# Row maxima of an attention kernel made 80 units ahead instead of 104, and some of their row transfers moved to ScalarE's queue

## The reference, cut to what matters

```python
xn = layernorm(x)                        # x: (2, 2048, 512)
q, k, v = split(xn @ W_qkv)              # 16 heads of 32
a = q @ k.T / sqrt(32) + alibi + causal  # per batch and head: 2048 x 2048
y = softmax(a) @ v
attn = y @ W_o
ffn = top-1 of 8 experts on xn           # gate * (xn @ W[e].T + b[e])
out = x + attn + ffn
```

## Time and profile before

| | us, or as said |
|---|---|
| median of 3 runs | 1774.7 (1774.01 to 1775.14) |
| the profiled execution | 1770.8 |
| its span | 1769.0 |
| PE busy | 1666.7 (94%) |
| DVE busy | 1045.4 (59%) |
| ACT busy | 761.1 (43%) |
| POOL busy | 675.0 (38%) |
| packets on ScalarE's queue q10 | 4608, for 32 y stores |
| idle of PEld until an exp of ACT | 86.4 in 365 waits, 0.8 the longest |

### The profile page before, as it was taken

The page is one execution under the profiler, slowest core; times in us unless marked ns, Lnnn a source line. Parts: engine busy times, 40 slices in busy tenths (PEclk is TensorE's granted clock), DMA queues, the critical chain, the costliest instruction groups (busy, mean ns, idle before and its releaser), DMA issues. The chain is left out here.

```text
span 1769.0 us, 27986 instructions
## 1 busy us (share of the span) xinstructions
PE 1666.7 (94%) x9970; PEld 1011.5 (57%) x9971; DVE 1045.4 (59%) x2452; ACT 761.1 (43%) x1575; POOL 675.0 (38%) x643
## 2 busy tenths in 40 slices
PE   5999999679999999999999999999999998799898
PEld 4777777444545545554555554554554533688686
DVE  5433332467777766776766776776776700634366
ACT  2222222114554654655655555555555564411110
POOL 4500000004862553553554454454355365223350
PEclk9999999859999999999999999999999999899999
DMA  6655564571803703702801801900900500545596
GB/s 228 215 180 184 178 205 147 161 127 39 157 8 71 124 8 65 137 8 53 148 8 41 160 8 30 171 8 20 182 8 8 202 7 13 173 143 164 189 395 229
DMA packets 96927, 203.59 MB, mean 115 GB/s; under 512 B 10908, under 2 KB 28348, under 8 KB 91164
## 3 DMA queue, kind: packets, MB, share of 16 engines
q1 hardware_dynamic: 82984, 170.17, 36.9%
q0 software_dynamic: 9216, 23.47, 4.2%
q10 hardware_dynamic: 4608, 8.39, 1.6%
HBM read 122.46 MB, written 79.01 MB: 114 GB/s over the span
## 5 line engine op out<-in xcount | busy, mean ns | idle before, releaser
L1037 ACT ACTIVATE probs_sb<-score_ps 128x512 f32<-128x512 f32 (+3 forms) x1280 | 595.1, 546 | 486.5 <-PE score_ps L1106 223.7
L916 POOL TENSOR_TENSOR pair_sum<-probs_sb 128x512 f32<-128x512 f32 x384 | 480.7, 1284 | 422.0 <-ACT probs_sb L1037 333.4
L939 DVE TENSOR_REDUCE part_max<-max_ps 128x1 f32<-128x512 f32 x768 | 476.0, 679 | 248.3 <-PE max_ps L1071 248.0
L1071 PE MATMUL max_ps<-k_aug,q_aug 104*128 104x512 f32 (+3 forms) x1280 | 531.4, 427 | 27.2 <-DMA q_aug<-q_rows_d 19.8
L1103 PE MATMUL score_ps<-q_aug,k_aug 106*128 106x512 f32 (+3 forms) x1280 | 475.2, 392 | 13.0 <-DMA q_aug<-max_lo 8.9
L1071 PEld LDWEIGHTS max_ps<-k_aug,q_aug 104*128 104x128 f32 x1280 | 250.7, 197 | 183.7 <-issue 80.4
L1103 PEld LDWEIGHTS score_ps<-q_aug,k_aug 106*128 106x128 f32 x1280 | 243.7, 191 | 114.4 <-ACT probs_sb L1037 86.4
L1148 PE MATMUL acc_ps<-probs_sb,v_sb 128*32 128x512 f32 (+3 forms) x2560 | 291.1, 534 | 0.0
L935 DVE CUSTOM_DVE_ANT_0 max_ps<-max_ps,mask_row 128x384 f32<-128x384 f32 (+3 forms) x512 | 238.8, 514 | 48.7 <-PE max_ps L1071 45.5
L1148 PEld LDWEIGHTS acc_ps<-probs_sb,v_sb 128*32 128x32 f32 x2560 | 73.0, 110 | 118.1 <-issue 91.3
L623 DVE SCALAR_TENSOR_TENSOR st_lo<-group_ps,st_hi 128x512 fp32r<-128x512 f32 x64 | 44.3, 692 | 139.9 <-ACT st_hi L670 139.9
(11 more groups left out here) (175 smaller groups left out, 1737.9 us busy)
## 6 DMA issues: line engine op xcount, KB each, us to landing
k_aug<-k_hi_d SPq DMA_DIRECT2D x14, 1024.0 KB
q_aug<-q_hi_d SPq DMA_DIRECT2D x14, 1024.0 KB
slot_y_d<-y_rows SPq DMA_DIRECT2D x39, 256.0 KB, 2.0
xn_d<-xn SPq DMA_DIRECT2D x8, 1024.0 KB, 5.4
q_hi_d<-st_hi SPq DMA_DIRECT2D x32, 256.0 KB, 3.4
q_lo_d<-st_lo SPq DMA_DIRECT2D x32, 256.0 KB, 3.9
k_hi_d<-st_hi SPq DMA_DIRECT2D x32, 256.0 KB, 2.5
k_lo_d<-st_lo SPq DMA_DIRECT2D x32, 256.0 KB, 2.8
```

The costliest lines, as they stand in the source:

```text
L916: nc.gpsimd.tensor_tensor(pair_sum[:, p % 2, hh], probs[:, s0, hh], probs[:, s1, hh], ALU.add).then_inc(pair_added, 1)
L939: nc.vector.tensor_reduce(part_max[:, hh * QT + i, kc:kc + 1], max_ps[:, bank, 0:w], AX.X, ALU.max).then_inc(max_taken, 1)
L1037: nc.scalar.activation(probs[:, r % P_SLOTS, hh, off:CH], score_ps[:, (r * HG + hh) % S_BANKS, off:CH], ACT.Exp).then_inc(exp_done, 1)
L1071: nc.tensor.matmul(max_ps[:, bank, 0:w], q_aug[0:ROW_MAX, half, hh, i * P:(i + 1) * P], k_aug[0:ROW_MAX, half, hh, kc * CH:kc * CH + w], s ...
```

## The change

AHEAD becomes 20. A middle group does its last 80 units (the last 16 of chunk 2 and all 64 of chunk 3) in rounds 0 to 19, and the first 80 of the next group in rounds 20 to 39; the first group does those 80 in rounds 21 to 39. Chains are now placed by done_by(), one round behind a chunk's last unit: in a middle group (0, 2) at round 4, (0, 3) at 20, (1, 0) at 24, (1, 1) at 32. The rows of chunk 2 are no longer in SP's queue: ScalarE issues them after the exps of the round that holds their SPLIT (round 5, in the first group round 10). The rows of group 0's chunk 0 also go to ScalarE's queue, ahead of its rounds.

```diff
-AHEAD = 14
+AHEAD = 20
 RATE = NMU // NR
 STREAM = units_of(1, *range(QC))
-EARLY = STREAM[:RATE * (NR - AHEAD)]
-LATE = [(0, UNIT, u) for _, _, u in STREAM[RATE * (NR - AHEAD):]]
-PLAN_MID = plan([spread(LATE, range(0, AHEAD)), spread(EARLY, range(AHEAD, NR))],
-                [(0, 3, AHEAD), (1, 0, AHEAD + 4), (1, 1, AHEAD + 12), (1, 2, AHEAD + 24)])
-PLAN_LAST = plan([spread(LATE, range(0, AHEAD))], [(0, 3, AHEAD)])
+NEARLY = RATE * (NR - AHEAD)
+EARLY = STREAM[:NEARLY]
+LATE = [(0, UNIT, u) for _, _, u in STREAM[NEARLY:]]
+
+def done_by(parts, dg, c):
+    rounds = [r for part in parts for r, events in part.items() if (dg, UNIT, OF_CHUNK[c][-1]) in events]
+    return [(dg, c, r + 1) for r in rounds]
+
+def with_chains(*parts):
+    return plan(parts, [chain for dg in (0, 1) for c in range(QC) for chain in done_by(parts, dg, c) if chain[2] < NR - 1])
+
+PLAN_MID = with_chains(spread(LATE, range(0, AHEAD)), spread(EARLY, range(AHEAD, NR)))
+PLAN_LAST = with_chains(spread(LATE, range(0, AHEAD)))
...
-PLAN_FIRST = plan([spread(units_of(0, 2), range(0, 9)), spread(units_of(0, 3), range(9, 21)),
-                   spread(units_of(1, 0, 1, 2), range(21, NR - 2)), spread(EARLY[OF_CHUNK[3][0]:], range(NR - 2, NR))],
-                  [(0, 1, 0), (0, 2, 9), (0, 3, 21), (1, 0, 24), (1, 1, 30), (1, 2, NR - 2)])
+PLAN_FIRST = with_chains({0: []}, spread(units_of(0, 2), range(0, 9)), spread(units_of(0, 3), range(9, 21)),
+                         spread(EARLY, range(21, NR)))
+PLAN_FIRST[0] = [(0, FOLD, 1), *PLAN_FIRST[0], (0, TURN, 1)]
+PLAN_FIRST[1] = [(0, SPLIT, 1), *PLAN_FIRST[1]]
...
 # SP: max_rows(g, 2), max_rows(g + 1, 2) and max_rows(0, 0, 0) go
...
 # ScalarE
+                def max_rows(g, cc, half):
+                    here = slice(cc * CH, (cc + 1) * CH)
+                    act.wait_ge(max_lo_done, g * QC + cc + 1)
+                    for row, part in ((ROW_MAX, max_hi), (ROW_MAX + 1, max_lo)):
+                        for hh in range(HG):
+                            act.dma_start(q_aug[row:row + 1, half, hh, here].bitcast(F32),
+                                          part[hh * TPC:(hh + 1) * TPC, cc % 2].bitcast(F32)).then_inc(max_rows_loaded[cc % 2], 16)
...
+                        if (0, SPLIT, 2) in events[r]:
+                            max_rows(g, 2, half)
                         if r in LEAVE_AT:
...
                 maxima(PLAN_BEFORE[0], BANKS_BEFORE, 0)
+
+                max_rows(0, 0, 0)
                 groups(act, step)
```

More of the change, by code:

```diff
@@ L858, in step @@
                     if first:
-                        max_rows(g, 2, half)
                         load(g + 1, 1 - half)
@@ L863, in step @@
                         max_rows(g + 1, 1, 1 - half)
-                        max_rows(g + 1, 2, 1 - half)
                         return
@@ L870, in step @@
                         max_rows(g + 1, 1, 1 - half)
-                    if not last:
-                        max_rows(g + 1, 2, 1 - half)
                 load(0, 0)
-                max_rows(0, 0, 0)
                 groups(sp, step)
```

## The result

The kernel after takes 1793.3 us (median of 4 runs, 1790.17 to 1793.83), the kernel before beside it 1774.9 (1774.01 to 1775.8): ratio 1.0104, 95% interval 1.0090 to 1.0117. It is slower by 18.4 us. The profiled execution took 1793.05 us, its span is 1791.3 (before: 1770.8 and 1769.0), so the traces have 22.3 us to explain. The page looks nearly as before; that is the first lesson, since a wait of 3 us in each of seven groups shows in no tenth of a slice.

A forecast was written before the change was run, and what follows sets the result against it. PE was taken as near full, with any ScalarE lateness passed on at once. Terms -8.9 - 11.6 + 1.1 - 3.0 + 26.1 + 10 = +13.7 on the profiled 1770.8 gave 1784.5, median about 1788, range 1763 to 1803.

The forecast's parts named there:

- First rows: Start of group 0: rows of maxima issued from ScalarE's queue remove PE's wait of 8.87 us, -8.9 us.
- Eight issues on ScalarE: Behind round 5, issues delay exps and PE by 3.4 us in seven groups, 2.3 in group 0: +26.1 us.
- rival B: Round 5: ScalarE's front end runs the issues beside queued exps, 0 to 0.7 us a group, about 1754; chance 0.18.
- The clock: Behind the eight waits: PE's granted clock falls after five of them, 2.0 us each, +10 us.
- Rival A: ScalarE's waits come but PE's clock holds: +3.7 us, 1778; chance 0.22.
- Units out of group 0: Rounds 20 to 39 of group 0: 24 units less at VectorE's 0.48 us each, -11.6 us.
- Last group: Rounds 14 to 19 of the last group take the 24 units: +1.1 us.
- The order: Groups 1 to 6: wide and narrow units change rounds, -0.5 us a group, -3 us in all.
- Rows landing: Round 12: with 17 us to land, rows issued by 580.1 arrive at 597, just in time.
- rival C: Rows land late beside the next group's load, 22 us, so PE waits at round 12: about 1808; chance 0.10.

The follow-up runs named there:

- e1: Kernel before, with only the rows of group 0's chunk 0 moved to ScalarE's queue: 1765.8 us, ratio 0.9955.
- e6: Kernel after, with chunk 2's rows back on SP, behind four of the load's nine transfers: 1757.9 us, ratio 0.9916.
- e3: Kernel after, with one maxima product of rounds 6 and 7 computed twelve times in groups 1 to 7: 1780.8 us, ratio 1.0038.
- e2: Kernel before, with chunk 3's eight rows issued by ScalarE after round 15 in groups 1 to 7, not by SP: 1797.4 us, ratio 1.0127.
- e4: Kernel after, with ScalarE's eight issues split in groups 1 to 7, four after round 5 and four after round 7: 1785.3 us, ratio 1.0068.
- e7: e6 with POOL's 32 token scatters moved within group 0, into rows of up to fourteen: 1774.2 us, ratio 0.9996.
- e10: e6 with POOL's scatters moved from group 0 to the last group, in rows of 10, 12 and 10: 1774.7 us, ratio 1.0006.
- e11: e6 with POOL's scatters moved from group 0 to groups 1 to 4, in rows of four: 1775.8 us, ratio 1.0011.
- e9: e6 with every maxima unit in group 0's rounds 8 to 11 computed twice: 1761.9 us, ratio 0.9939.
- e5: Kernel after, with chunk 2's rows back on SP, ahead of the whole load of the next group: 1761.0 us, ratio 0.9919.
- e12: e11 with the first four transfers of group 1's load issued ahead of the rows of chunk 2: 1770.1 us, ratio 0.9975.

## Why the prediction was right, and where its terms were not

The forecast, 1788 us (1763 to 1803), has the right sign and mechanism; the result is 5 us above it. In terms of the profiled executions +13.7 stood against +22.3; part of the nearness of 1788 is that the execution profiled before the change lay 3.9 us below its median and the one after it 0.2. Step by step:

- **First rows, -8.9.** e1 gave -8.9 (8.7 in its trace); in the kernel after the stretch is 8.0 shorter. Right.
- **Eight issues on ScalarE, 7 x 3.4 + 2.3.** e6 and e3 give 3.1 a group, 21.8 together. The record is 0.580 us an issue, as taken over from SP's 0.573; the first costs nothing as one exp is still queued. In group 0 rounds 10 and 11 grew by 1.5 us and rounds 12 and 13 by 0.7, of which PE waits 0.55 for the rows. Right, if 2.2 us too dear in sum; rival B, that the front end runs the issues beside the exps, is dead: the 4.37 us are put down to issue.
- **The clock, +10.** The mechanism was right and the size nearly: 11.5 us, by e3. That it came so near is in part luck, since count and price were off in opposite ways: I took five falls at 2.0 us; the granted clock fell behind each of the seven waits in groups 1 to 7 (0.57 to 0.60 over the 4 us behind it), at 1.6 us each. Behind comparable waits it fell in five of seven groups of e2 and three of six of e4; no run gives a rule for the count. The first stretch of group 1 also ran in a fall, 14.52 us against 12.89. Rival A, that the clock holds, is ruled out.
- **Units out of group 0, -11.6.** It was -9.2. The rate of 0.48 us a unit was VectorE's; with fewer units rounds 28 and 29 became POOL's (PE waits 1.76 us for an exp that waits for its slot behind pair sums and scatters), and stay at 8.37 where e7 and e10 have 6.66. That was next late, and I had not named it.
- **Last group, +1.1.** Rounds 14 to 19 grew by 1.6; with the issue stretch (4.8) and a fall of the clock in rounds 24 and 25 (6.52 us at 0.76, 5.07 in e6) the group is 8.2 longer.
- **The order, -3.** This term failed. What it counted was right: rounds 14 and 15 lost 0.36 (5.82 to 6.18), rounds 20 to 23, 26 and 27 gained 0.98. What it left out was not nothing: in the middle groups rounds 0 to 3 went from 11.91 to 12.89 and rounds 4 and 5 from 5.43 to 5.88, while other rounds gained, and groups 1 to 6 differ by 0.1 us in e6.
- **The 8.6 us by which the sum fell short** are then: the clock 4.6 (1.5, and 3.1 in two falls away from the issues), the order 3.1, the units 2.4, the first rows 0.9, the last group's rounds 0.5, less 2.2 that the issues came out under, less 0.7 in the rest, for which no run gives a cause.
- **Rows landing.** No wait at round 12 in groups 1 to 7, as the forecast had it; e4 shows that 7.5 us less between the last issue and round 12 bring rival C, and that about 5 us were to spare. I gave it 0.10, and it was nearer than that.

The Trainium skill (DMA: Bandwidth & Descriptors, "Issuing engines are not separate DMA queues") says that issuing from several engines saves only the sequencer's time to start a DMA, which is usually small relative to the DMA itself. The prediction took that as a price near nothing and the trace as against it. The comparison as the Trainium skill makes it holds here: an issue takes 0.58 us, and in e4 the rows needed 15.6 to 17.5 us behind the last one to land. It is not the comparison that decides: eight issues in a row keep ScalarE from its exps, and PE waits for those.

The other half of that section of the Trainium skill, that DMAs started by any engine run on the same 16 DMA engines and interleave, agrees with e4. Rows on ScalarE's own queue came late beside the load on SP's (10.6 us of waits; in group 1 the DMA share between the low rows' issue and round 12 is 1.06). In the last group, which loads no next group, that share is 0.07, and 14.9 us behind the last issue PE waited for nothing.

One reading of the prediction was incomplete, and the clock term hung on it, its only evidence that a wait brings a fall. It took the fall of the clock in rounds 10 and 11 of group 0 for the effect of a 1.03 us wait on VectorE. In e6 that stretch takes 12.87 us at 0.73; with the scatters out of group 0 (e11) 9.39 at 1.00; with the scatters in place and PE given more work (e9) 10.34 at 1.00. So the scatters start it, and with them in place 2.5 of the 3.5 us came back when more work held the clock. That the term's mechanism held for ScalarE's waits was shown by e3, not by this stretch. A smaller slip: groups 1 to 6 of the kernel before repeat at 135.1 to 135.4 us, not to within 0.1; no term used it.

## What to carry to other kernels

Before moving DMA issues to another engine's queue, multiply them by the issue time of one (0.57 to 0.58 us here, 0.61 from one to the next) and ask whether that engine has so long a gap; ScalarE had one of over 20 us ahead of its first exp (worth 8.9) and none so long in the groups (cost 3.1 each, plus 1.6 of clock). To bring a small transfer forward, reorder it within the queue that has time: on SP, ahead of the bulk load (e5) or after four of its nine transfers (e6), it held up no round. And a change with two parts of opposite sign is to be run in parts; here one part alone was worth 0.45% and the rest buried it.

## What the runs showed of the hardware that was not expected

- More work on TensorE made the kernel faster: eleven useless products a group kept the clock at 1.00 through the wait, and the kernel took 12.4 us less (e3).
- POOL's indirect scatters (0.97 us each, 1.27 apart) can slow all other engines: 12 to 14 us for 7.8 behind a row of four, 23.9 for 9.4 beside one of fourteen, with the DMA engines 1% busy in e12's stretch. Every stretch hit has narrow tiles, but not every such stretch beside scatters is hit (rounds 22 and 23 of group 0 in e6: four scatters, 7.80 us). The records call the gaps "remote" and "issue"; what is contended was not tested and stays open.
- In one to three groups of the profiled executions of the kernel after, e3, e4, e5 and e10 the first four rounds take 14.5 us for 12.9, at a clock of 0.88, in e6 never. No run tells why; it is 3.3 of the 7.0 us between the profiled executions of e5 and e6.
